# Graph network, 16 graphs: input norm, dots and masks moved to steps 3 to 5 of a pair, the final attention to steps 0 to 3, b2 folded into a column bias

## The reference

```python
h = relu(layernorm(x))                       # per token
mask = adj + eye > 0
for l in range(3):                           # D = 256, 4 * D = 1024
    si, sj = h @ attn_w[l, :D], h @ attn_w[l, D:]
    scores = leaky(si[:, :, None] + sj[:, None, :] + attn_b[l], 0.2)
    attn = softmax(where(mask, scores, -inf), axis=-1)
    y = layernorm(h + attn @ h) * g1[l] + beta1[l]
    ff = gelu(y @ W1[l] + b1[l]) @ W2[l] + b2[l]
    h = layernorm(y + ff) * g2[l] + beta2[l]
x = x + h
g = relu(layernorm(x)); Wh = g @ W           # final graph attention, W (256, 256)
e = leaky(Wh @ a1 + (Wh @ a2).T, 0.2)
att = softmax(where(adj > 0, e, -9e15), axis=1)
out = x + leaky(att @ Wh, 0.2)
```

## Time and profile before

| | |
|---|---|
| three runs | 2317.78 us median, 2314.73 to 2318.89 |
| the profiled execution | 2312.36 us, span of its instructions 2310.6 us |
| busy: PE, DVE, ACT, POOL | 1937.2, 1697.3, 1166.5, 915.7 us |
| mean granted clock of TensorE | 0.959 of 2.4 GHz |
| HBM | 42.36 MB read, 8.39 MB written, 22 GB/s |

### The profile page before, as it was taken

One profiled execution on the slowest core, in us unless ns is written; L12 is line 12 of the kernel. 1 busy time (PEld: TensorE's weight loads), 2 busy tenths in 40 slices (PEclk: granted clock), 3 DMA queues, 4 the chain that ended last, 5 costly groups with the idle time before them and its releaser, 6 DMA issues.

```text
span 2310.6 us, 34337 instructions
## 1 busy us (share of the span) xinstructions
PE 1937.2 (84%) x11201; PEld 1651.7 (71%) x11201; DVE 1697.3 (73%) x5031; ACT 1166.5 (50%) x1844; POOL 915.7 (40%) x661
## 2 busy tenths in 40 slices
PE   3888888997789978899778987889878898879994
PEld 2777676886678867787667776678767786668873
DVE  6666788667786777867777777776787767876655
ACT  2554555454555545555445554555545555555542
POOL 2345433443334443344333443334333444334442
PEclk9899989999999999999999999999989999999997
DMA  4001100001000010001000010000100001000000
GB/s 153 19 19 46 42 6 10 19 19 46 7 14 10 19 46 11 19 1 38 28 11 19 1 55 11 10 19 1 56 11 10 19 19 42 5 10 28 1 1 19
DMA packets 40909, 53.15 MB, mean 23 GB/s; under 512 B 2920, under 2 KB 31244, under 8 KB 40716
## 3 DMA queue, kind: packets, MB, share of 16 engines
q1 hardware_dynamic: 40716, 50.76, 6.7%
HBM read 42.36 MB, written 8.39 MB: 22 GB/s over the span
## 4 chain that ended last, share of the span: by engine, by line
PE 35%; issue 27%; POOL 16%; DVE 15%; ACT 5%; DMA 1%; POOLq 0%; SPq 0%; ACTq 0%; DVEq 0%
PE ps_d L470 11%; PE ps_a L405 9%; POOL gelu_lo L1207 5%; PE ps_u L444 5%; POOL x_nat L1183 3%; PE ps_a L500 2%; POOL probs L1213 2%; DVE junk L937 2%; ACT normed L652 2%; PE ps_t L414 2%; DVE probs L1009 2%; POOL rstd L1174 2%; ACT g_full L671 2%; PE ps_a L486 1%; PE ps_u L428 1%
## 5 line engine op out<-in xcount | busy, mean ns | idle before, releaser
L671 ACT ACTIVATE g_full<-ps_u,vec_col 128x512 f32<-128x512 f32 x384 | 258.6, 686 | 494.5 <-PE ps_u L444 269.2
L470 PE MATMUL ps_d<-w_hi,gelu_hi 128*128 128x256 f32 x1536 | 460.4, 300 | 37.2 <-POOL gelu_lo L1207 27.6
L470 PE MATMUL ps_d<-w_hi,gelu_lo 128*128 128x256 f32 x1536 | 439.7, 286 | 0.0
L470 PE MATMUL ps_d<-w_lo,gelu_hi 128*128 128x256 f32 x1536 | 438.9, 286 | 0.0
L1174 POOL TENSOR_TENSOR rstd<-var_eps,minus_half 128x4 f32<-128x4 f32 x128 | 135.4, 1058 | 695.3 <-DVE var_eps L795 695.3
L405 PE MATMUL ps_a<-x_nat,probs 128*128 128x257 f32 x1536 | 364.0, 390 | 36.4 <-DVE normed L880 33.5
L1207 POOL TENSOR_TENSOR gelu_lo<-g_full,gelu_hi 128x512 fp32r<-128x512 f32 x240 | 310.4, 1302 | 175.9 <-ACT gelu_hi L679 161.6
L405 PEld LDWEIGHTS ps_a<-x_nat,probs 128*128 128x128 f32 x1536 | 286.0, 192 | 107.9 <-DVE normed L880 42.4
L470 PEld LDWEIGHTS ps_d<-w_hi,gelu_hi 128*128 128x128 f32 x1536 | 299.1, 195 | 55.2 <-POOL gelu_lo L1207 38.3
L470 PEld LDWEIGHTS ps_d<-w_lo,gelu_hi 128*128 128x128 f32 x1536 | 297.4, 194 | 6.0
L470 PEld LDWEIGHTS ps_d<-w_hi,gelu_lo 128*128 128x128 f32 x1536 | 296.9, 193 | 0.0
(11 more groups left out here) (135 smaller groups left out, 3827.4 us busy)
## 6 DMA issues: line engine op xcount, KB each, us to landing
adj_in<-adj_dram SPq DMA_DIRECT2D x64, 256.0 KB, 2.9
x_nat<-x_dram SPq DMA_DIRECT2D x16, 512.0 KB, 4.0
x_res<-x_dram SPq DMA_DIRECT2D x16, 512.0 KB, 3.9
out_dram<-x_res SPq DMA_DIRECT2D x64, 128.0 KB, 1.7
x_res<-L_gnn_W_dram SPq DMA_DIRECT2D x5, 1024.0 KB, 5.2
probs<-L_gnn_W_dram SPq DMA_DIRECT2D x1, 1024.0 KB, 11.3
attn_row<-L_gnn_attn_w_dram SPq DMA_DIRECT2D x1, 768.0 KB
g_row<-L_gnn_g_dram SPq DMA_DIRECT2D x1, 384.0 KB
```

The lines of the kernel that those rows point to most:

```text
L470: last = pe.matmul(ps_d[c // 2][:, cols:cols + D], h[:, r, tok], w[:, layer, f, :], start=False, stop=(f == FC - 1 and i == 2), skip_group ...
L671: full = act.activation(g_full[:, f % 2, :], ps_u[f % 2][:, :], ACT.Gelu, bias=b1_col[:, layer, f:f + 1])
```

## The change

- The side 0 graph's final attention begins in step 0 of the next pair and ends in step 1; that of side 1 begins in step 2 and ends in step 3. Steps 4 and 5 have none. `mask_g` has room for both sides; a graph's is made in its own pair (side 0 in step 2, side 1 in step 5, in the last pair in step 4), behind `neighbour_max`.
- Input norm, apply and dots of the next pair are done in step 4 (side 0) and step 5 (side 1), for the attention two steps on. They have their own root tile `rstd_x`. Statistics stand before `attention_sum`, the shift in it after chunk 0, the dots behind `attention_norm`; ACT's `input_apply` stands between gelus 5 and 6.
- Masks of side 0: chunks 0 and 1 in step 3, 2 and 3 in step 4. Side 1: all four in step 5, before `bounded_scores`; the transposes of side 1 now in step 5, as those of side 0 in step 4.
- In steps 0 and 5 the scores row is turned right behind `up_first`. A step with a final begin has `down(4)`, `up(7)` and `down(5)` between the attention and the projection. The last step has its own function, `closing_slot`, which turns and projects after `up(5)` and `down(3)`, and ACT's final copies stand before gelus 6 and 7.
- b2: the four matmuls L457 and their setup go. `both_col` = beta1 + b2 is the bias of `h_full`, and `h_rest` subtracts b2 again.
- Many small tiles become columns of one tile.

```diff
-mask_g = sb("mask_g", [P, NC, N], BF16)
+mask_g = sb("mask_g", [P, 2, NC, N], BF16)
...
+        self.n, self.side, self.layer, self.other = pair * STEPS + k, side, layer, 1 - side
+        self.begins = first and k == 0
+        self.attend = not (last and k == STEPS - 1)
+        self.layer_a = (layer + side) % LAYERS
+        self.first_x = pair * 2 + 1 if self.begins else None
+        self.ff_graph = None
+        if k == STEPS - 1:
+            self.ff_graph = pair * 2
+        if k == 0 and not first:
+            self.ff_graph = pair * 2 - 1
+        self.final = None
+        if not first and k == 0:
+            self.final = (pair * 2 - 2, 0, self.n - 2)
+        if not first and k == 2:
+            self.final = (pair * 2 - 1, 1, self.n - 3)
+        self.late = None
+        if not first and k == 1:
+            self.late = (pair * 2 - 2, 0)
+        if not first and k == 3:
+            self.late = (pair * 2 - 1, 1)
+        self.keep = {2: (pair * 2, 0), 5 if not last else 4: (pair * 2 + 1, 1)}.get(k)
+        self.early_masks = (pair * 2 + 2, 0) if k == 3 and not last else None
+        self.prepare = pair * 2 + 2 + side if layer == LAST and not last else None
+        self.turn = pair * (STEPS - 2) + k - 1
...
+            if s.early_masks is not None:
+                load_adjacency(s.early_masks[0], (0, 1))
+            if s.late is not None:
+                store(*s.late)
+            if first and s.n + 2 < len(weight_loads):
+                load_weights(s.n + 2)
+            if s.layer == LAST:
+                if first and s.side == 0:
                     sp.wait_ge(w_low.sem, w_low.at(len(weight_loads) - 1))
-                load_residual(pair, side)
-            if prepare is not None:
-                load_input(prepare, side, n)
+                load_residual(pair, s.side)
+            if s.prepare is not None:
+                load_input(s.prepare, s.side, s.n)
+                load_adjacency(s.prepare, (2, 3))
+                if s.side == 0:
+                    load_adjacency(s.prepare + 1, (0, 1))
...
-        pe.matmul(dst[:, cols:cols + D], ones_r[:, :], b2_parts[:, layer, :], start=False, stop=False,
-                  skip_group_check=True)
...
+    def slot(s):
+        n, layer = s.n, s.layer
         up_first(n, layer)
+        pe.wait_ge(h_act.sem, h_act.at(n))
+        rows_soon = s.layer_a == 0 and not s.begins
+        if rows_soon:
+            scores_row(n + 1)
         up(n, layer, 2)
         up(n, layer, 3)
         down(n, layer, 0)
-        pe.wait_ge(h_act.sem, h_act.at(n))
-        if late is None:
+        if s.late is None and not rows_soon:
             scores_row(n + 1)
         down(n, layer, 1)
         up(n, layer, 4)
-        if late is not None:
+        if s.late is not None:
             scores_row(n + 1)
-            final_out(late, range(NC))
+            final_out(s.late[0], range(NC))
         down(n, layer, 2)
         bound_rows(n + 1)
         up(n, layer, 5)
         down(n, layer, 3)
         up(n, layer, 6)
-        attend_out(n + 1, 1 - side, layer_a, graph_a, late)
+        attend_out(n + 1, s.other, s.layer_a, pair_graph(s), s.late[0] if s.late is not None else None)
         pe.wait_ge(q_ready.sem, q_ready.at(n + 1))
-        if prepare is None:
-            down(n, layer, 4)
-            up(n, layer, 7)
-            down(n, layer, 5)
-        else:
-            down(n, layer, 4)
-            mask_transposes(prepare, 0, (0, 1))
-            up(n, layer, 7)
-            mask_transposes(prepare, 0, (2, 3))
-            down(n, layer, 5)
-            pe.wait_ge(mask_ready.sem, mask_ready.at(prepare))
+        down(n, layer, 4)
+        if s.final is not None:
+            turn_tokens(wh, lng_apply, g_tr, s.final[0])
+        if s.prepare is not None:
+            mask_transposes(s.prepare, s.side, (0, 1))
+        up(n, layer, 7)
+        if s.prepare is not None:
+            mask_transposes(s.prepare, s.side, (2, 3))
+        down(n, layer, 5)
+        if s.prepare is not None:
+            pe.wait_ge(mask_ready.sem, mask_ready.at(s.prepare))
+        if s.final is not None:
+            project(s.final[0], n + 1)
+            final_rows(s.final[0])
         turn_tokens(normed, ln1_apply, h_tr, n + 1)
         down(n, layer, 6)
         down(n, layer, 7)
...
+            low_row(n + 1)
+            exps(n + 1)
+            gelu(n, layer, 5)
+            if s.prepare is not None:
+                input_apply(s.prepare, s.side)
             gelu(n, layer, 6)
-            if final is not None:
-                final_h(final)
-            if masks_x is not None:
-                mask_copies(masks_x, 0, (0, 1))
+            if s.final is not None:
+                final_h(s.final[0])
+            if s.prepare is not None:
+                mask_copies(s.prepare, s.side, (0, 1))
             gelu(n, layer, 7)
-            if masks_x is not None:
-                mask_copies(masks_x, 0, (2, 3))
-            if final is not None:
-                final_wh(final)
-                final_low(final)
-            if attend:
-                h_split(n + 1, layer_a)
+            if s.prepare is not None:
+                mask_copies(s.prepare, s.side, (2, 3))
+            if s.final is not None:
+                final_wh(s.final[0])
+                final_low(s.final[0])
+            h_split(n + 1, s.layer_a)
...
-            act.activation(h_full[:, k, :], ps_t[k][:, :], ACT.Identity, bias=beta1_col[:, layer, k:k + 1],
+            act.activation(h_full[:, k, :], ps_t[k][:, :], ACT.Identity, bias=both_col[:, layer, k:k + 1],
...
-            dve.tensor_tensor(h_lo[:, k, :], h_full[:, k, :],
-                              h_hi[:, k, :].bitcast(F32), ALU.subtract).then_inc(h_ready.sem, 1)
+            dve.scalar_tensor_tensor(out=h_lo[:, k, :], in0=h_full[:, k, :], scalar=b2_col[:, layer, k:k + 1],
+                                     in1=h_hi[:, k, :].bitcast(F32), op0=ALU.subtract,
+                                     op1=ALU.subtract).then_inc(h_ready.sem, 1)
...
+        for s in slots(pair, first, last):
+            n = s.n
+            if s.begins:
+                gelu_high(n)
+                input_stats(s.first_x, 1, 0)
+                gelu_rest(n, 1)
+                input_shift(s.first_x)
+                layer_scores(n + 1, 1, s.first_x)
             else:
+                ff_norm(n - 1, (0, 1) if s.late is not None else (0,),
+                        (n + 1, s.layer_a, s.turn) if s.layer_a > 0 else None)
+            if s.late is not None:
+                final_bounded(s.late[0], s.late[1], 2)
+                final_scale(s.late[0])
+            elif not s.begins:
                 gelu_rest(n, 1)
+            if not s.attend:
                 gelu_rest(n, 3)
+                gelu_rest(n, 4)
+                final_norm(s.ff_graph, 0, n - 1)
+                final_apply(s.ff_graph, 0, range(NC))
+                final_begin(s.ff_graph, 0, n)
+                continue
+            if s.prepare is not None and s.side == 0:
+                prepare_masks(s.prepare, 0, (2,))
+            neighbour_max(n + 1, s.other)
+            if s.keep is not None:
+                final_mask(*s.keep)
+            if s.late is not None:
+                final_leaky(s.late[0], range(NC))
+            if s.prepare is not None and s.side == 1:
+                prepare_masks(s.prepare, 1, (0,))
+            gelu_rest(n, 3)
+            if s.prepare is not None:
+                prepare_masks(s.prepare, s.side, (3,) if s.side == 0 else (1,))
             gelu_rest(n, 4)
+            if s.prepare is not None and s.side == 1:
+                prepare_masks(s.prepare, 1, (2, 3))
+            bounded_scores(n + 1, s.other, s.late[0] if s.late is not None else None)
+            if s.final is not None:
+                final_norm(*s.final)
+            if s.early_masks is not None:
+                prepare_masks(s.early_masks[0], s.early_masks[1], (0,))
+            if s.prepare is not None:
+                input_stats(s.prepare, s.side, pair + 1)
+            if s.ff_graph is not None:
+                dve.wait_ge(x_ready.sem, x_ready.at(n - 1))
+            attention_sum(n + 1, s.other, s.final, s.prepare)
+            attention_norm(n + 1)
+            if s.prepare is not None:
+                layer_scores(n + 2, s.side, s.prepare)
+            if s.early_masks is not None:
+                prepare_masks(s.early_masks[0], s.early_masks[1], (1,))
+            if s.final is not None:
+                final_begin(s.final[0], s.final[1], n + 1)
+            h_rest(n + 1, s.layer_a)
...
     ff_norm(B * LAYERS - 1)
-    final_bounded(B - 2, 2)
-    final_mask(B - 1, 1)
+    final_bounded(B - 2, 0, 2)
     final_scale(B - 2)
...
+            if s.ff_graph is not None:
+                layer_input(n - 1, s.other, LAST, n)
             else:
+                if not s.begins:
+                    layer_input(n - 1, s.other, s.layer - 1 + s.side)
                 gelu_rest(n, 2)
```

(10 more changed lines are left out.)

320 lines of the change are left out of this document (92 added, 228 removed).

## The result

| | before | after |
|---|---|---|
| median of the runs | 2317.22 us (4 runs, 2314.73 to 2318.89) | 2245.87 us (4 runs, 2244.08 to 2248.39) |
| profiled execution, span | 2312.36, 2310.6 us | 2248.39, 2246.6 us |

The ratio is 0.9698, 95% interval 0.9683 to 0.9712: faster by 71 us.

The account below looks back on a forecast made before the run. PE, busiest at 84%, was near no limit; its waits for DVE chains, partly held by POOL, were the target. Middle pairs -28, first pair -9, last +2 gave -35: 2283 us, own range 2268 to 2295, eight in ten 2248 to 2318.

Parts of the forecast that it names:

- Step 0: Middle pair's step losing late half, input norm, dots and mask copies: 46.3 us against 62.1, -15.8.
- S: Start of a step's first bounded-score instruction, from the step's start; forecast +20.0, +19.5, +23.3 in steps 0, 4, 5.
- Step 4: Middle pair's step gaining input statistics, shift and dots, with two mask chunks instead of four: 42.0 us against 42.3, -0.3.
- Step 2: Middle pair's step getting the odd graph's final norm, projection and rows, and the kept mask: 44.6 us against 36.3, +8.3.
- Steps 1 and 3: Middle pair's steps holding the final attention's late half: 47.3 us each; step 3 +11.0 from 36.3, step 1 unchanged.
- first rival: Clock falls in steps 1 and 3 as the `wh` wait grows: 0.9 to 1.6 us a step, 2296 to 2305; chance 0.17.
- Step 5: Middle pair's step losing the dots wait and final work, gaining kept mask and four chunks: 47.5 us against 55.4, -7.9.
- The 6.83 us wait: PE's largest wait, in step 5 before the neighbour scores row, for DVE's dots of the next pair; forecast gone.
- fourth rival: Steps 2 and 3 take what steps 5 and 0 give (+19.3 against -23.7); pair comes out even: 2310; chance 0.08.
- b2 at 0: Dropping four b2 matmuls a step gains 0, since they stand before waits other chains end; far bound 38 us.
- second rival: Holds are light or PE sets more: 2 us a pair in steps 4 and 5 each, a third of b2; 2255; chance 0.16.
- The third, step 5's queue: DVE's queue before step 5's scores runs late: gain gone from 5 us on, 2339 at 8 us; chance 0.12.

Follow-up runs that it names:

- Experiment 4: Changed kernel with DVE's side 1 dots behind `h_rest` instead of ahead of it in step 5: 2264.77 us, ratio 0.9756 to the kernel before.
- experiment 5: Changed kernel with the six middle pairs written out instead of looped: 2233.22 us, ratio 0.9644 to the kernel before.
- experiment 8: Changed kernel with side 1's kept mask made in step 4 behind the bounded scores instead of in step 5: 2259.55 us, ratio 0.9759 to the kernel before.
- experiment 3: Changed kernel with input statistics, shift, apply and dots put back to the heads of steps 5 and 0: 2349.95 us, ratio 1.012 to the kernel before.
- experiment 2: Changed kernel with four matmuls a step put back in b2's place, with other operands: 2251.52 us, ratio 0.9698 to the kernel before.
- experiment 9: Kernel before, middle pairs written out, without the four b2 matmuls a step: 2295.22 us, ratio 0.9889 to the kernel before.

## Why the prediction was right or wrong

From profile to profile the spans differ by 64.0 us where 35 were forecast; the other 7 of the 71 are the two profiled executions, the fastest of its kernel before and the slowest after. The 64.0 are 1.5 of setup (forecast 2.5), 4.7 in the first pair (6.5), 56.7 in the six middle pairs (28) and 1.1 in the last (-2). So the term that failed is the sum of a middle pair: -9.45 on average instead of -4.7. Over the six middle pairs step 0 is 4.0 us under its forecast, steps 2 and 4 are 1.3 under, and steps 1 and 3 are 0.8 and 0.9 over. (The last pair's terms, as the prediction lists them, add up to +2.8 and not to +2.)

- **Step 0, 42.4 instead of 46.3, is where it failed**: 3.9 of the 5.2 us of pair 3, in two terms. *S at +17.3, not +20.0.* I took "DVE still starts late at the loop's seam (885.26, 3.9 after the start)" from the earlier trace rows. But that start was 3.0 us behind DVE's own last instruction, and the change itself takes `final_begin` from the end of step 5. DVE's statistics begin at +2.3, still 3.10 of issue behind its queue's end, and PE waits 0.17 and 0.69 us for the applied norm and not "some 3 us". Experiment 4 moves the same start back and loses 2.4 us in step 0. And the sums were not held "until about +18": they were through at +14.0, since the hold that caught them was L1172's and not L1174's, which caught only a gelu rest, up to +17.4. *S to the fourth chunk 9.84 us, not 10.9* (884.75 less 874.91): the two first `final_apply` instructions took 1.70 where they had taken 2.62 beside POOL's gelu rests, in the row below of the kernel before. This second term I read from the trace alone.

```profile
1143.52 2.62 DVE L981 TENSOR_SCALAR wh<-x_res,mean,rstd 128x256 f32<-128x256 f32 x2
```

- **Step 4, 40.7 instead of 42.0**: the mask chunk and a sum were held as forecast (2.36 and 2.04), S came at +18.8 instead of +19.5, and the "blocked shift (1.25)" took 0.16, since POOL had no instruction running at 1065.4. *Step 2, 43.3 instead of 44.6*: S was right (+18.1), the offset again 9.8.
- **Steps 1 and 3** had the right form: 47.4 and 48.4 against 47.3, the 1.1 of step 3 being the first rival's, below.
- **Step 5 was right in part by luck**: 47.6 against 47.5, S at +23.3 as worked out, and PE's wait before the attention (4.04) within "3 to 5". But the same hold was misread as in step 0: the sums were not "ready at +15.5" but at +13.3 (1093.06), with L1172's end, and L1174 held the kept mask instead, which cost 3.8 us (0.68 and 3.14) and not 1.9. The two misses cancel, and the four mask chunks behind took what was forecast. In the written-out kernel of experiment 5 the sums are held to L1174's end, at +15.5, and S comes out at +22.9: which instruction is caught changed, what the lock cost at S hardly did. How fine that is shows in the kernel of experiment 8: in pairs 1 and 2 the first sum of step 5 begins at +9.59 and is not held, in pairs 3 to 5 it begins at +9.63 or +9.64 and is, and the sums are through at +13.4 and at +15.7.
- **The 6.83 us wait** was the right thing to look at, and experiment 3 shows its size: undone, the change is slower than before. That all else costs 28 us by itself is the "moved, not removed" of the fourth rival, and the reason why the sum was a small difference of large terms; a miss of 4 us in one step doubled it.
- **b2 at 0** held within what the runs can tell: 0 to 6 us by experiment 2, a few and at most some 13 by experiment 9. PE's busy time fell by 27 us, as the lower bound of 27 to 38 has it, and the span did not follow.
- **Rivals.** The first, the clock, came true, and its price per step was right: in nine of the twelve steps 1 and 3 of the middle pairs the 1.2 GHz level follows the wait for `wh`, 48.2 to 48.5 us instead of 47.3, some 10 us in all (step 3 above: wait 3.43, granted clock 0.96, and one stretch of 32 matmuls in 8.86 us). It did not decide, since the other steps gained more. Its reason, that b2's absence lengthens the wait, is only half right: the wait grew by 0.2 us and not 0.5 to 0.8, and experiment 2, with four matmuls a step back and a wait of 3.20, has as many such steps. In two of the other three the wait is 2.06 and 2.11; in step 1 of pair 3, one of these, the level was low ahead of the wait (granted clock 0.74 from 910 to 916 us) and full behind it. What picks the steps is not settled. The second rival, 2255, has the nearest number and the wrong reasons: b2 does not show, step 5 gained nothing over the forecast, and the sums and the kept mask were held. The third, step 5's queue, did not happen at +23.3; the load of chunk 3 came 0.82 us late and not 3.
- **The range.** Its low end of 2248 came from rival 2. Its terms do not give its number: 2 us a pair in steps 4 and 5 each are 28 us in seven pairs, not 14, and with the 12 for b2 they lead from 2283 to 2243, not to 2255. The range took no bound for step 0's start at the seam, which I had treated as known since a row showed it, though the sentence that gave the 3.9 also gave its 3.04 of issue. With the other 0.9 us taken as open, about 6 us in seven pairs, the low end would have been some 2242 and have held the time.
